# A GNN kernel: attention sums stored densely in edge order, and gathered by the node update

## What is computed

```
logits = jnp.sum(q[dst] * (k[src] + e_k), axis=-1) * scale + es_tab[edge_type]
logits = logits + jnp.clip(jnp.log(eg_tab[edge_type]), -10.0, 10.0)
mx = jax.ops.segment_max(logits, dst, num_segments=n)
ex = jnp.exp(logits - mx[dst])
sums = jax.ops.segment_sum(ex, dst, num_segments=n)
attn = ex / jnp.maximum(sums[dst], 1e-12)
msg = (v[src] + e_v) * attn[..., None]
agg = jax.ops.segment_sum(msg.reshape(-1, nh * hd), dst, num_segments=n)
agg = agg @ Wo + bo
agg = agg * (1.0 + 0.5 * jnp.tanh(gamma))[None, :] + beta[None, :]
x = _layer_norm(node_embeddings + agg, ln1_g, ln1_b)
h = jax.nn.gelu(x @ W1 + b1, approximate=False) @ W2 + b2
return _layer_norm(x + h, ln2_g, ln2_b)
```

## Time and profile before

| | us |
|---|---|
| median of 3 runs | 5455.94 (5452.72 to 5460.40) |
| the profiled execution, its own time | 5462.3 |
| its span, first to last instruction | 5460.5 |

### The profile page before, as it was taken

How to read it: one execution, slowest core, us unless ns; L and a number is a source line. 1 busy time by engine, 2 the same in 40 slices (tenths; PEclk the granted TensorE clock), 3 DMA queues, 4 the chain that set the end, 5 groups by cost and what they waited for, 6 DMA issues and landing times. The chain is left out here.

```text
span 5460.5 us, 58163 instructions
## 1 busy us (share of the span) xinstructions
PE 3428.0 (63%) x12060; PEld 2054.0 (38%) x12060; DVE 2713.5 (50%) x6625; ACT 1084.0 (20%) x2025; POOL 2798.6 (51%) x2360
## 2 busy tenths in 40 slices
PE   3664735555995887756767658777735555555534
PEld 1222524444774665532222225555522222222212
DVE  6997731111455222655455436777754444444423
ACT  0232411111221111222222213333311111111100
POOL 0463058885114861337777751122128888787740
PEclk7776655555555555555555555555557777677765
DMA  4222621111552111541111121121112222233210
GB/s 186 93 69 88 262 74 23 23 23 25 146 162 75 22 19 48 194 143 23 23 24 23 23 56 75 68 101 67 74 54 31 29 30 29 28 30 30 27 16 3
DMA packets 350981, 346.67 MB, mean 63 GB/s; under 512 B 264934, under 2 KB 290266, under 8 KB 350834
## 3 DMA queue, kind: packets, MB, share of 16 engines
q1 hardware_dynamic: 229596, 272.37, 15.2%
q0 software_dynamic: 107888, 60.13, 9.1%
q10 hardware_dynamic: 13350, 12.40, 0.7%
HBM read 172.86 MB, written 175.50 MB: 64 GB/s over the span
## 5 line engine op out<-in xcount | busy, mean ns | idle before, releaser
L842 PE MATMUL e_ps<-e_msg,e_hot 128*128 x2408 | 597.9, 425 | 326.5 <-POOL e_msg L753 231.7
L842 PEld LDWEIGHTS e_ps<-e_msg,e_hot 128*128 128x128 f32 x2408 | 539.4, 326 | 431.2 <-issue 431.2
L2227 POOL DMA_INDIRECT out<-d_out,d_end x356 | 591.2, 1661 | 172.1 <-issue 167.1
L2271 PE MATMUL d_pl<-d_hot,d_fields 128*65 128x512 f32 x712 | 504.6, 875 | 0.0
L814 DVE TENSOR_TENSOR e_ps<-e_ps,e_before 128x65 f32<-128x65 f32 (+1 forms) x172 | 40.0, 233 | 793.2 <-PE e_ps L842 793.2
L1990 POOL DMA_INDIRECT list<-s_rec,s_place x200 | 199.1, 995 | 288.2 <-DVE s_place L1906 231.3
L734 POOL DMA_INDIRECT e_msg<-from_src,e_src x200 | 194.7, 973 | 292.9 <-DMA e_first<-lot_first 238.5
L1328 PE MATMUL u_po<-bias_parts,ones 3*128 3x256 bf16 x392 | 148.7, 379 | 215.9 <-issue 95.9
L1690 POOL TENSOR_TENSOR u_tg<-u_t,norms 128x1792 f32<-128x1792 f32 x14 | 55.5, 3963 | 444.7 <-DVE u_t L1525 444.7
L739 POOL DMA_INDIRECT e_msg<-h1d,e_src x200 | 221.1, 1105 | 102.0 <-issue 54.8
L934 POOL DMA_INDIRECT a_ends<-h,a_src x200 | 220.8, 1104 | 102.5 <-issue 60.6
(11 more groups left out here) (359 smaller groups left out, 8142.1 us busy)
## 6 DMA issues: line engine op xcount, KB each, us to landing
u_z<-h SPq DMA_DIRECT2D x28, 896.0 KB, 6.2
x<-sums SPq DMA_DIRECT2D x28, 896.0 KB, 7.8
u_x<-x SPq DMA_DIRECT2D x28, 896.0 KB, 7.3
terms<-s_zeros SPq DMA_DIRECT2D x16, 812.5 KB, 12.8
s_key_row<-src_key SPq DMA_DIRECT2D x50, 256.0 KB, 3.0
h1d<-u_h SPq DMA_DIRECT2D x14, 910.0 KB, 9.4
u_z<-h1d SPq DMA_DIRECT2D x14, 910.0 KB, 4.5
term<-u_h SPq DMA_DIRECT2D x14, 910.0 KB, 3.6
```

What stands on the lines that cost most here:

```text
L842: last = nc.tensor.matmul(to, hot[s][:, q, :], rows, start=False, stop=q == LOT - 1)
L2227: pool.indirect_dma_start(net.out[:, :], bass.IndirectOffsetOnAxis(ap=end[s][:, j:j + 1], axis=0), out[s][:, j, 0:C], None, bounds_check=N ...
L2271: last = nc.tensor.matmul(pl[0:WEIGHT + 1, :], fields[:, j, :], hot[:, j, :], start=j == 0, stop=j == J - 1)
```

## The change

The sums of every edge are stored, and each node reads one row.

- `agg2` and its zeroing are gone, and with them `end` and the scatters. `attended` has one row of zeros (row 0) and then a row for each edge of the list. SP's `store` writes `out` of a chunk there, in one plain transfer of 128 KB.
- In `node_update` for layer 0, `last_edges` computes `dst_end`, one index for each of the 50176 node rows: the place of the node's last edge in the list (counted from 1), or 0 for a node without an edge. It takes a 64 KB load, two matmuls of 392 columns and nine DVE instructions.
- In `node_update` for layer 2, A is no longer loaded: POOL's `gather` issues 28 indirect transfers for a super-tile, and PE waits for each sub-tile's 4. POOL's code is written out instead of looped.

```diff
@@ -912,16 +911,29 @@
                     after = net.dst_rows[bass.ds(c * CH + J, CH)].rearrange("(p j) -> p j", j=J)
                     sp.dma_start(dst[s][:, J:J + 2], after[:, 0:2]).then_inc(loaded[s], 16)
                     sp.dma_start(etype[s][:, :], rows_4(net.etype, c)).then_inc(loaded[s], 16)
+                def store(t, s):
+                    sp.wait_ge(out_ready, 2 * t + s + 1)
+                    rows = net.attended[bass.ds((2 * t + s) * CH + 1, CH), :].rearrange("(p j) c -> p j c", j=J)
+                    sp.dma_start(rows, out[s][:, :, :]).then_inc(stored[s], 16)
                 for s in range(2):
                     load(s, s)
-                with sp.Fori(1, CHUNKS // 2) as t:
+
+                def next_load(t, s):
+                    sp.wait_ge(gathered[s], 16 * 2 * J * t)
+                    sp.wait_ge(flags, 2 * t + s - 1)
+                    sp.wait_ge(onehot_ready, 2 * t + s - 1)
+                    load(2 * t + s, s)
+                for s in range(2):
+                    next_load(1, s)
+                with sp.Fori(2, CHUNKS // 2) as t:
                     for s in range(2):
-
-
-                        sp.wait_ge(gathered[s], 16 * 2 * J * t)
-                        sp.wait_ge(flags, 2 * t + s - 1)
-                        sp.wait_ge(onehot_ready, 2 * t + s - 1)
-                        load(2 * t + s, s)
+                        store(t - 2, s)
+                        next_load(t, s)
+                for t in (LAST - 1, LAST):
+                    for s in range(2):
+                        store(t, s)
+                for s in range(2):
+                    sp.wait_ge(stored[s], 16 * (CHUNKS // 2))
             @block.gpsimd
             def _(pool):
...
@@ -934,22 +946,11 @@
                             pool.indirect_dma_start(ends[s][:, j, half * C:(half + 1) * C], None, net.h2[:, :],
                                                     bass.IndirectOffsetOnAxis(ap=rows, axis=0)).then_inc(gathered[s], 16)
-                def scatter(t, s):
-                    pool.wait_ge(out_ready, 2 * t + s + 1)
-                    pool.sem_inc(pool_turn, 1)
-                    for j in range(J):
-                        pool.indirect_dma_start(net.agg2[:, :], bass.IndirectOffsetOnAxis(ap=end[s][:, j:j + 1], axis=0),
-                                                out[s][:, j, :], None, bounds_check=NP - 1, oob_is_err=False).then_inc(scattered[s], 16)
                 for s in range(2):
                     gather(0, s)
                 with pool.Fori(0, LAST) as t:
                     for s in range(2):
                         gather(t + 1, s)
-                        scatter(t, s)
-                for s in range(2):
-                    scatter(LAST, s)
-                for s in range(2):
-                    pool.wait_ge(scattered[s], 16 * J * (CHUNKS // 2))
             @block.tensor
             def _(pe):
...
@@ -1064,13 +1065,7 @@
                                             net.iota8[:, :, :], ALU.is_equal).then_inc(onehot_ready, 1)
                 def make_flags(t, s):
-
-                    v.wait_ge(scattered[s], 16 * J * t)
-                    nc.vector.tensor_tensor(fresh[s][:, :], dst[s][:, 1:J + 1], dst[s][:, 0:J], ALU.not_equal)
-                    nc.vector.tensor_tensor(same[:, :], dst[s][:, 1:J + 1], dst[s][:, 2:J + 2], ALU.is_equal)
-                    v.drain()
-                    nc.vector.scalar_tensor_tensor(end[s][:, :], same[:, :], float(FAR), dst[s][:, 1:J + 1],
-                                                   ALU.mult, ALU.add).then_inc(flags, 1)
+                    nc.vector.tensor_tensor(fresh[s][:, :], dst[s][:, 1:J + 1], dst[s][:, 0:J], ALU.not_equal).then_inc(flags, 1)
                 def products(t, s):
                     k = 2 * t + s + 1
...
@@ -1112,6 +1107,7 @@
                     v.drain()
                     nc.vector.reciprocal(dsum[:, :, :], dsum[:, :, :])
                     v.drain()
+                    v.wait_ge(stored[s], 16 * t)
                     for j in range(J):
                         last = nc.vector.tensor_tensor(
                             out[s][:, j, :].rearrange("p (h d) -> p h d", d=HD),
...
@@ -1217,7 +1222,7 @@
         x_out = (net.x1, net.x2, net.out)[layer]
         h_out = (net.h1d, net.h2, net.term0)[layer]
         LAST = SUPER - 1
-        in_loads = 2
+        in_loads = 2 if layer < 2 else 1
         def summed(number, columns=slice(0, C)):
...
@@ -1328,11 +1333,15 @@
                     nc.tensor.matmul(po[b][:, 0:J * C], net.ones3[:, :],
                                      net.bias_parts[:, which, :, :].rearrange("k j c -> k (j c)"), start=True, stop=False)
-                def products(source, phase, start=False):
+                def products(source, phase, start=False, ready=None):
+                    if ready is not None:
+                        ready(0)
                     turn(source, phase, 0, start)
                     for i in range(SUBS):
                         q, b = phase[0] * SUBS + i, (phase[1] + i) % 2
                         if i + 1 < SUBS:
+                            if ready is not None:
+                                ready(i + 1)
                             turn(source, phase, i + 1, start)
                         pe.wait_ge(zt_ready, q + 1)
                         if not start or i > 1:
...
@@ -1379,6 +1388,11 @@
                         if i + 2 < SUBS:
                             turn(T[s], phase, i + 2, False)
                         down(i)
+                if layer == 0:
+                    pe.wait_ge(lanes_loaded, 16)
+                    pe.wait_ge(edges_copied, 1)
+                    nc.tensor.matmul(in_tile[:, 0:TILES], earlier_lane[:, :], edges_of[:, :], start=True, stop=True)
+                    nc.tensor.matmul(of_tile[:, 0:TILES], all_lanes[:, :], edges_of[:, :], start=True, stop=True).then_inc(edges_summed, 1)
                 if layer < 2:
                     def step(c, start=False):
                         pe.wait_ge(z_ready, c[0] + 1)
...
@@ -1390,8 +1404,9 @@
                     step(at(0, LAST))
                 else:
                     def attend(c, phase, start=False):
-                        pe.wait_ge(loaded[c[1]], 16 * in_loads * (c[2] + 1))
-                        products(A[c[1]], phase, start)
+                        def ready(i):
+                            pe.wait_ge(gathered[c[1]][i], 16 * J * (c[2] + 1))
+                        products(A[c[1]], phase, start, ready)
                     attend(at(0, 0), FIRST_PHASE, True)
                     attend(at(0, 1), attend_phase(at(0, 1)))
                     mlp(at(0, 0), mlp_phase(at(0, 0)))
...
@@ -1580,9 +1595,26 @@
                                 roots(after)
                         v.drain()
                         v.sem_inc(inputs_used, 1)
+                    def last_edges():
+                        v.wait_ge(edges_summed, 1)
+                        nc.vector.tensor_tensor_scan(upto[:, :], ones_t[:, :], of_tile[:, 0:TILES], 0.0, ALU.mult, ALU.add)
+                        nc.vector.tensor_scalar(has_edge[:, :], edges_of[:, :], 0.0, None, ALU.is_gt)
+                        nc.vector.tensor_tensor(edges_of[:, :], edges_of[:, :], in_tile[:, 0:TILES], ALU.add)
+                        v.drain()
+                        nc.vector.tensor_tensor(upto[:, :], upto[:, :], of_tile[:, 0:TILES], ALU.subtract)
+                        v.drain()
+                        nc.vector.tensor_tensor(upto[:, :], upto[:, :], edges_of[:, :], ALU.add)
+                        v.drain()
+                        nc.vector.tensor_tensor(net.dst_end[:, :], upto[:, :], has_edge[:, :], ALU.mult)
                     if layer == 0:
+                        nc.vector.memset(all_lanes[:, :], 1.0)
+                        nc.vector.memset(ones_t[:, :], 1.0)
+                        nc.vector.tensor_copy(edges_of[:, :], sums[:, 0:TILES, C])
+                        v.drain()
+                        v.sem_inc(edges_copied, 1)
                         counts(at(0, 0))
                         roots(at(0, 0))
+                        last_edges()
                     step(at(0, 0), after=at(0, 1))
                     with v.Fori(0, SUPER // 2 - 1) as t:
                         for d in (1, 2):
...
@@ -1700,15 +1732,27 @@
                         number, s, h = c
                         pool.wait_ge(normed, number + 1)
                         nc.gpsimd.tensor_tensor(X[s][:, :, :], X[s][:, :, :], H[s][:, :, 0:C], ALU.add).then_inc(tail_ready, 1)
-                    offset(at(0, 0))
-                    gained(at(0, 0))
-                    offset(at(0, 1))
-                    gained(at(0, 1))
-                    with pool.Fori(0, SUPER // 2 - 1) as t:
-                        for d in (2, 3):
-                            gained(at(t, d))
-                            tail(at(t, d - 2))
-                            offset(at(t, d))
+
+                    def gather(c):
```

(25 more changed lines are left out.)

20 lines of the change are left out of this document (14 added, 6 removed).

## The result

| | before | changed |
|---|---|---|
| median of 4 runs, us | 5458.17 (5452.72 to 5462.03) | 5312.33 (5301.23 to 5317.69) |
| ratio | | 0.9737, 95% interval 0.9724 to 0.9749 |
| the profiled execution, us | 5462.3 | 5317.69 |
| its span, us | 5460.5 | 5315.9 |

A forecast was written before the change was run, and what follows sets the result against it. POOL's indirect transfers bound attention_sums, the chain PE, ACT, DVE layer 2's node_update. Terms -170 + 60 + 7 + 0 = -103 took the profiled 5462.3 to 5359, the median 6 lower: 5353 us, range 5300 to 5415.

The forecast's parts named there:

- the forecast's own case: PE bounds attention at 12.4 us a chunk, POOL the node update at about 57 a super-tile; 5320 to 5390, chance 0.60.
- the second case: Layer 2 node update: DVE doesn't stall the gathers, which hide; only the first fill of +23 stays; 5316 us, chance 0.15.
- The attention, -170: attention_sums: without scatters on POOL, PE bounds a chunk at 12.4 us instead of 15.84; 165 us saved, 5 more at the end.
- the third case: Attention: TensorE's clock rises as PE stays busy, POOL then bounds the chunk; 58 us less, 5295; chance 0.04.
- The node update, +60: Layer 2 node_update: gathers make POOL the bound, 57 us a super-tile over 53.25; attend(13) done at S + 742, not S + 681.
- The stalls: Layer 2 node update: gathers starting under two-input SBUF instructions of DVE wait; some 7 a period, 1.2 to 1.3 us each.
- The slower case (0.08): Layer 2 node update: gathers bound by many reads of row 0; at 2.2 us a gather, +325, 5618 us; chance 0.08.
- The attention keeping half of its waits (0.08): Attention: load-and-gather chain over 4 us longer than counted, chunk 14.1 us; +82, 5435 us; chance 0.08.
- Layer 0, +7: Layer 0 node_update: new matmuls wait for a 64 KB load behind four large ones, delaying PE's first transposes; 4 to 12 us.
- The zeroing, 0: Zeroing of agg2 dropped: 12.8 MB less written, but DVE is busy with one-hot tables and nothing waits; 0 us.

The follow-up runs named there:

- The run with reductions: Changed kernel with three two-operand SBUF instructions of DVE in layer 2's node_update replaced by one-operand reductions of the same tile size; 5299.1 us, ratio 0.9713.

## Why the prediction was right, point by point

The sign, the mechanisms of the sum and the range held; 5353 was 41 us too high against the median, and 5312 lies just below the 5320 to 5390 that I had given the forecast's own case. It is 4 us from the 5316 of the second case by chance: there the gathers aren't stalled and the old period holds, and neither was so. Nor is the sum as good as its total. The attention gave 50 us more than I had, and the node update took 16 more.

- **The attention, -170: mis-sized, -220.** Chunk for chunk the forecast held: 11.87 and 12.75 us in turn at 1.2 GHz, against "11.95" and "12.8". The count of chunks times the mean period gives the parts: before 15.93 us (I took 15.84 from one chunk), after 11.62, and 12.31 if all had run at 1.2 GHz. So 49 x 3.62 = 177 us are the mechanism (forecast 165), 49 x 0.69 = 34 the clock, and 9 the ends of the stage, of which I had 5. The step that failed is the third case, to which I gave 0.04: the clock did rise, in 15 short stretches, 51 us in all (3 and 10 us before), and shortened 15 of 49 chunks to 9.6 to 10.4 us, where I had let it rise everywhere or nowhere. The evidence I set against it, 2 us at 0.50, was of another stage, and PE had begun its transposes there only 2.8 us before, after a wait of 15.9, so it could say little of a whole stage. The Trainium skill (TensorE: Matmul & The Clock Gate, Part 1) has 2.4 GHz follow sustained activity. The traces agree in direction (mean 0.51 with PE busy 67% of the stage, 0.54 with 86%), but not in size, with 0.50 in chunks in which PE was busy for 11 of 12 us.
- **The node update, +60: mis-sized, +76.** The start was right: gained(0) begins at S + 78 (forecast 77, with its end at 81), 37 us later than before. The periods were 57.47 where I had 57, over ten of them 41 us. The gathers stall as forecast, but 8 in a period for 1.4 us each (37.6 - 28 x 0.944, over 8), where I took 7 for 1.2 to 1.3; the 1 to 2 us that I had allowed for POOL's waits on DVE did not come. The first two periods added 6 and the last took back 9. What I had wrong was the end of the old stage: PE begins the last transposes of `attended` at S + 668 there, not near S + 681 as I had worked out from one `gained`; in the changed kernel at S + 749, forecast 742.
- **The stalls.** The second case (they don't happen, 0.15) rested on the inference of the Trainium skill (SBUF — State Buffer, Who interferes with whom) that writing descriptors doesn't suffer from `tensor_tensor`. For these indirect transfers the traces say otherwise: 93 of 392 gathers were long, each of those ending 0.81 us after a DVE instruction with two operands in SBUF, and those that began under reductions, or under additions that read one operand from PSUM, took 0.94 to 0.96. The run with reductions took the stalls of the three replaced instructions away.
- **The slower case (0.08)**: its premise was half right, one row that many read lands 0.8 us later; its price was 6 us at most, since POOL issues a gather each 1.25 us and the landing lies beside that.
- **The attention keeping half of its waits (0.08)** fell: PE's wait for `a_ends` is 2.7 us. POOL does wait for its loads, 29 times, up to 2.9 us, which uses up slack that it has.
- **Layer 0, +7**: +7.7 in the stage, 5.7 of it between z and the first transposes, at a granted clock of 0.51 before and 0.50 after. With the same code there and a clock of 0.52 to 0.53, in three other runs, the stage took 350 to 352 us, about as long as before, so the 2 us beyond the 5.7 may be the clock's. **The zeroing, 0**: `sort_by_source` has not moved.
